# Merged stage: every group's routing stands ahead of the next group's logarithms and mixing

## The reference, cut to what matters

```
no = max(o, u + k);   y = (exp(o-no)*p + exp(u+k-no)*v) / (exp(o-no)*q + exp(u+k-no))
no2 = max(w + o, k);  p, q, o = exp(w+o-no2)*p + exp(k-no2)*v, exp(w+o-no2)*q + exp(k-no2), no2
```

```
probs = softmax(layernorm(x) @ gate.T);  w, idx = top_k(probs, 8);  w = w / sum(w)
out = sum over the chosen e of w_e * (silu(x @ Wgate_e) * (x @ Wup_e)) @ Wdown_e
```

## Time and profile before

| | us |
|---|---|
| median of 3 runs | 2035.82 (2034.09 to 2037.69) |
| the profiled execution | 2036.18 |
| its span, first to last instruction | 2034.5 |
| PE busy | 1671.5 (82%) |
| DVE busy | 1139.8 (56%) |
| POOL busy | 1044.0 (51%) |
| ACT busy | 791.4 (39%) |

### The profile page before, as it was taken

One profiled execution on the slowest core, in us unless ns is written; L12 is line 12 of the kernel. 1 busy time (PEld: TensorE's weight loads), 2 busy tenths in 40 slices (PEclk: granted clock), 3 DMA queues, 4 the chain that ended last, 5 costly groups with the idle time before them and its releaser, 6 DMA issues. The chain is left out here.

```text
span 2034.5 us, 36281 instructions
## 1 busy us (share of the span) xinstructions
PE 1671.5 (82%) x9306; PEld 1233.2 (61%) x9306; DVE 1139.8 (56%) x3459; ACT 791.4 (39%) x2192; POOL 1044.0 (51%) x1023
## 2 busy tenths in 40 slices
PE   7988985888699999999996576564159999999982
PEld 3466663555377777777773233332149988888872
DVE  3122335665544566666665666776425567777774
ACT  3411222222144454554544334333025554445541
POOL 5040006577763333333331267777777666666652
PEclk9999996998899999999997787766579999999996
DMA  8836647993476778778433137334956678888884
GB/s 302 261 95 155 167 126 250 361 333 114 142 286 229 264 278 284 271 274 292 160 131 112 55 112 271 126 125 139 389 164 200 194 245 268 289 269 290 287 266 166
DMA packets 244105, 444.72 MB, mean 219 GB/s; under 512 B 92560, under 2 KB 174608, under 8 KB 241168
## 3 DMA queue, kind: packets, MB, share of 16 engines
q1 hardware_dynamic: 168352, 237.46, 36.4%
q0 software_dynamic: 47856, 147.81, 19.9%
q10 hardware_dynamic: 27712, 57.28, 8.4%
HBM read 281.09 MB, written 237.60 MB: 255 GB/s over the span
## 5 line engine op out<-in xcount | busy, mean ns | idle before, releaser
L1044 PE MATMUL ps<-w_all,h_xT 128*128 x2112 | 551.4, 384 | 0.3 <-ACT h_xT L1328 0.3
L1061 PE MATMUL ps<-w_all,h_hT 89*128 (+1 forms) x1472 | 411.5, 384 | 27.0 <-DVE h_y L1924 24.8
L795 POOL DMA_INDIRECT y_b<-h_y,h_ix x314 | 316.8, 1009 | 164.6 <-issue 112.5
L1044 PEld LDWEIGHTS ps<-w_all,h_xT 128*128 128x128 f32 x2112 | 348.0, 193 | 48.1 <-issue 3.9
L795 POOL DMA_INDIRECT y_a<-h_y,h_ix x208 | 202.2, 972 | 302.0 <-ACT h_y L1361 287.4
L779 POOL DMA_INDIRECT xs_b<-h_x,slot_of x256 | 269.5, 1053 | 160.4 <-DVE slot_of L1755 83.1
L1061 PEld LDWEIGHTS ps<-w_all,h_hT 89*128 89x128 f32 (+1 forms) x1472 | 271.1, 192 | 90.3 <-issue 34.4
L1328 ACT COPY h_xT<-ps 128x256 f32<-128x256 f32 x528 | 194.4, 368 | 196.7 <-PE ps L1037 193.7
L779 POOL DMA_INDIRECT xs_a<-h_x,slot_of x192 | 191.7, 999 | 119.0 <-issue 57.9
L1037 PE MATMUL ps<-ident,h_x 128*128 128x128 f32 x912 | 178.4, 277 | 29.3 <-DMA h_x<-xs_b 29.1
L1037 PEld LDWEIGHTS ps<-ident,h_x 128*128 128x128 f32 x912 | 128.4, 143 | 82.7 <-issue 20.1
(11 more groups left out here) (266 smaller groups left out, 2235.0 us busy)
## 6 DMA issues: line engine op xcount, KB each, us to landing
xs_b<-void_d SPq DMA_DIRECT2D x40, 1128.0 KB
h_x<-xs_b SPq DMA_DIRECT2D x80, 564.0 KB
h_c<-y_a ACTq DMA_DIRECT2D x28, 768.0 KB, 5.3
h_x<-xs_a SPq DMA_DIRECT2D x34, 564.0 KB, 4.2
xs_a<-void_d ACTq DMA_DIRECT2D x16, 1128.0 KB, 13.6
w_all<-in_exp SPq DMA_DIRECT2D x6, 2560.0 KB, 22.2
h_x<-y_b SPq DMA_DIRECT2D x28, 512.0 KB
s_b<-y_b SPq DMA_DIRECT2D x28, 512.0 KB
```

The lines of the kernel that those rows point to most:

```text
L795: pool.indirect_dma_start(y_d[L.name], bass.IndirectOffsetOnAxis(ap=h_ix[:, i % IX:i % IX + 1], axis=0), result_buffer(L, i), None).then_i ...
L1044: m = pe.matmul(ps[:, 2 + s % 2, 0:2 * L.H], h_xT[:, s % 2, c, :], w_all[:, bass.ds(e * L.W + c * 2 * L.H, 2 * L.H)], start=(c == 0), stop ...
L1061: m = pe.matmul(ps[:, 6 + s % 2, 0:D], h_hT[0:w, s % 2, j, :], w_all[0:w, bass.ds(e * L.W + L.up0 + j * D, D)], start=(j == 0), stop=(j == ...
```

## The change

It changes the order of the three lists. In passes 1 to 7 of all engines the routing of group g-1 now stands where group 0's stood: DVE's choice between the two `weight_sums` and its slots ahead of `mixed`; ACT's row steps, turning and exponential around the second `decays`; PE's turning and logits ahead of `past_less_key` and its ranks directly behind. Group 7's routing in pass 8 keeps its order. `last_choices_summed` and `last_choices_added` move from pass 2 to pass 3, and PE's wait in it from `wk_yu` 2 to 3. A wait is added: `states_back(3)` waits for `wk_var` 2. ACT's `key_deviations(2, ...)` stays in pass 3. No instruction of an engine or queue is added or removed by the source except this wait; SP's and POOL's lists are unchanged.

```diff
--- before.py
+++ after.py
@@ -1100,7 +1100,7 @@
 
             def last_choices_summed():
                 pe.wait_ge(k_in, 16)
-                pe.wait_ge(wk_yu, 2)
+                pe.wait_ge(wk_yu, 3)
                 for h in range(2):
                     for k in range(L0.K):
                         m = pe.matmul(ps[:, h, :], ident[:], k_a[:, 2 * h:2 * h + 2, k * D:(k + 1) * D],
@@ -1134,6 +1134,8 @@
                 pe.wait_ge(wk_y, g + 1)
                 if g:
                     pe.wait_ge(wk_yu, g)
+                if g == 3:
+                    pe.wait_ge(wk_var, 2)
                 for j in range(GT):
                     for c in range(KC):
                         m = pe.transpose(ps[:, j // 2, (j % 2) * D + c * P:(j % 2) * D + c * P + P],
@@ -1148,22 +1150,22 @@
                 if g < NG:
                     decays_of(g, 0)
                     decays_of(g, 1)
-                if g == 1:
-                    turned(L1, 0)
-                    logits(L1, 0, e_g1)
+                if 0 < g < NG:
+                    turned(L1, g - 1)
+                    logits(L1, g - 1, e_g1)
                 if g < NG:
                     past_less_key(g, 0)
                     past_less_key(g, 1)
-                if g == 1:
-                    ranks(L1, 0)
-                if g == 2:
+                if 0 < g < NG:
+                    ranks(L1, g - 1)
+                if g == 3:
                     last_choices_summed()
-                if g > 1:
+                if g == NG:
                     turned(L1, g - 1)
                     logits(L1, g - 1, e_g1)
                 if g + 1 < NG:
                     keys_turned(g + 1)
-                if g > 1:
+                if g == NG:
                     ranks(L1, g - 1)
             experts_of_tiles(L1, 2)
             end_stage(pe, "M")
@@ -1456,29 +1458,30 @@
             for g in range(NG + 1):
                 if g < NG:
                     decays(g, 0)
-                if g == 1:
-                    row_logarithms(0)
-                    row_deviations(0)
-                    rows_normalised(0)
-                    results_landed(act, L0)
-                    turned(L1, 0)
+                if 0 < g < NG:
+                    row_logarithms(g - 1)
+                    row_deviations(g - 1)
+                    rows_normalised(g - 1)
+                    if g == 1:
+                        results_landed(act, L0)
+                    turned(L1, g - 1)
                 if g < NG:
                     decays(g, 1)
-                if g == 1:
-                    exponentials_of(L1, 0)
+                if 0 < g < NG:
+                    exponentials_of(L1, g - 1)
                 if g < NG:
                     logarithms(g, 0)
                     logarithms(g, 1)
-                if g > 1:
+                if g == NG:
                     row_logarithms(g - 1)
                     row_deviations(g - 1)
                 if g < NG:
                     shares(g, 0)
-                if g > 1:
+                if g == NG:
                     rows_normalised(g - 1)
                 if g < NG:
                     shares(g, 1)
-                if g > 1:
+                if g == NG:
                     turned(L1, g - 1)
                     exponentials_of(L1, g - 1)
                 if g == 3:
@@ -2126,26 +2129,26 @@
                     residual(g - 1)
                 if g < NG:
                     weight_sums(g, 0)
-                if g == 1:
-                    row_tails(0)
-                    row_scales(0)
-                    less_largest(L1, 0)
-                    chosen_experts(L1, 0)
+                if 0 < g < NG:
+                    row_tails(g - 1)
+                    row_scales(g - 1)
+                    less_largest(L1, g - 1)
+                    chosen_experts(L1, g - 1)
                 if g < NG:
                     weight_sums(g, 1)
-                if g == 1:
-                    slots_of(L1, 0)
-                if g > 1:
+                if 0 < g < NG:
+                    slots_of(L1, g - 1)
+                if g == NG:
                     row_tails(g - 1)
                     row_scales(g - 1)
                 if g < NG:
                     mixed(g, 0)
                     mixed(g, 1)
-                if g == 2:
+                if g == 3:
                     last_choices_added()
                 if g == 4:
                     key_scales(2, slice(NT - GT, NT))
-                if g > 1:
+                if g == NG:
                     less_largest(L1, g - 1)
                     chosen_experts(L1, g - 1)
                     slots_of(L1, g - 1)
```

## The result

| | before | after |
|---|---|---|
| median, us | 2035.55 (2034.09 to 2037.69, 4 runs) | 2057.91 (2054.35 to 2060.95, 4 runs) |
| ratio to before | | 1.0098 (95% interval 1.0074 to 1.0122) |
| profiled execution's span, us | 2034.5 | 2059.2 |
| pass 1 to pass 2, scans of `largest` | 47.60 | 47.60 |
| pass 3 to pass 4 | 43.2 | 56.8 |

The prediction was 2056.5. The profiled execution of after reaches pass 1 3.9 us later than that of before (1120.58 against 1116.67), in stages that the change doesn't touch; its time, 2060.95, is the highest of its four. So times in stage M are compared here from the start of pass 1.

The account below looks back on a forecast made before the run. It saw hand-over idling in the merged stage and POOL's dispatch holding up H1. Passes (285.6) and last choices (10.9) put residual(7) 46.6 us and POOL 22.5 later, H1 20.7 later: 2056.5 us against the median, range 2042 to 2070.

Parts of the forecast that it names:

- Six passes at 47.60: Merged stage: passes 2 to 7 each take pass 1's measured 47.60 us, together 285.6 us.
- The clock case: PE's clock: all at 2.4 GHz, passes of 44.6 us, 2038.5 (chance 0.11); all at 1.2 GHz, 50.9 us, 2076 (0.09).
- The last choices: 3.9 + 6.7 + 0.3: Passes 3 and 4: moved step 3.9 us, exposed key chain 6.7 (at least 5.3), key_scales 0.3; together 10.9 us.
- `residual(7)` 46.6 later: End of pass 7: residual(7) starts at 1462.6 against 1415.97, including 1.8 us waiting for states_back(7).
- POOL 22.5 later: POOL drains each group and idles, only the last two count; first H1 result at 1537.0 against 1514.51.
- The 1.6 us for stores beside the mixing: POOL's group 6: 1.6 us added for four slower issues beside DVE's mixing, at least 0, at most 5.
- The stall at result 14 from 25.2 to 1.1: H1: result 14 wanted at 1546.1, gets its buffer at 1547.2; the 25.2 us stall shrinks to 1.1.
- The sum 20.7 us: Whole kernel: H1's hidden layers end 20.7 us later, the rest moves with them; 2056.5 against the median.
- the 7.90 us per pass: Merged stage: early order costs 7.90 us of idle time per pass, pass 1's 47.60 against pass 7's 39.70.
- the two waits it named: DVE in pass 1: 8.1 us waiting for PE's logits and 4.0 us for the ranks.
- the rival with short passes: Merged stage: POOL's gap is filled and passes take 43 us, giving 2028 us; chance of faster 0.07.

Follow-up runs that it names:

- e1: Changed kernel with ACT's key_deviations(2) moved from pass 3 to pass 4; 2055.53 us, ratio to before 1.0086.
- e3: Changed kernel with three more waited-for stores on SP ahead of the six weight loads, putting off PE's start of H1; 2064.74 us, ratio to before 1.0136.
- e4: Kernel before with three more waited-for stores on SP ahead of the six weight loads, putting off PE's start of H1; 2035.52 us, ratio 1.0001.
- e9: Changed kernel with PE's ranks moved ahead of past_less_key in passes 1 to 7, nothing else; 2030.71 us, ratio to before 0.9967.
- e8: Kernel of e6 with ACT's logarithms also moved ahead of the routing's exponential; 2027.94 us, ratio to before 0.9962.
- e6: Changed kernel with DVE's second weight_sums moved ahead of less_largest and chosen_experts in passes 1 to 7; 2052.22 us, ratio to before 1.0064.

## Why the prediction was right

- *Six passes at 47.60.* Measured 47.6, 47.6, 47.9, 47.3, 47.7 for passes 1, 2, 4, 5 and 6 between scans. The clock case didn't come: the logit matmuls took 3.67 us in pass 7 and the waits stayed 7.8 to 9.0.
- *The last choices: 3.9 + 6.7 + 0.3.* Pass 3 was 9.2 us over 47.6. The exposed wait was 5.37, close to its stated low end of 5.3, since the table load ran ahead of the wait; e1 took it away and gave 5.2 back. With `key_scales` the term was 9.5 us, 1.4 less than the 10.9 of the sum.
- *`residual(7)` 46.6 later.* 45.0; its wait for the transposes was 2.11, taken as 1.8.
- *POOL 22.5 later.* 21.4. That it drains before each group, and that only the last two count, was seen. The 1.6 us for stores beside the mixing measured 2.15 (four stores of 1.30 to 1.88). The count has a small slip: 32 x 1.27 is 40.6, not 40.8.
- *The stall at result 14 from 25.2 to 1.1.* 2.89. Result 14 was wanted 44.6 us later than before, not 46.6, and got its buffer 22.3 later, not 22.5: the difference is the 1.8 us. On POOL's side two errors nearly cancel, which is luck: the first result came 1.1 us earlier than forecast, and the buffer 0.9 us later behind it than in before; why is open. e3 and e4 tested the slack by itself.
- *The sum 20.7 us.* From the start of pass 1 to the end of the span the two profiled executions differ by 20.8 (938.6 against 917.8), so the stages come out as added up. The medians differ by 22.4; the ratio's interval leaves 4.9 us either way, so the 1.7 between them is not clear of noise.

What the prediction did not have was the cause of the 7.90 us per pass in parts, and the 7.90 itself was read from one short pass: old passes 3 to 7 took 43.2, 40.3, 39.8, 41.9 and 39.8 us, 41.0 on the mean, so the early order cost 6.6. The forecast didn't need it, since it counted passes of 47.60. Of the two waits it named, 8.1 and 4.0 us, the second was a matter of order, not of work: PE's order alone (e9) or DVE's and ACT's together (e8, against e6) removes it, and e9's passes average 42.8, 4.8 less than after's 47.6. The first wait was not turned to use in any run: in e8 1.4 us are left of it, but a wait of 5.7 for `w_e` came up, and its passes, 42.7 on the mean, are about as long as e9's. Where the last 1.8 us per pass go, and whether e8 and e9 together would gain more, was not tested. e9 also bears out the price of the rival with short passes: at 43 us a pass it said 2028, and e9 took 2030.71.

## What to carry to other kernels

Work put earlier in the list of an engine that runs in order also goes ahead of everything behind it: for each moved step, list what it waits for and what then waits behind it, on every engine. A consumer with a fixed number of equal jobs (here 256 stores of POOL) loses time mainly by its start and its gaps; find the first point that waits for its last job, and judge the producer's order by that, not by when the producer ends, as long as the other limit keeps its slack (e4 against e3). When a result is made later, look for the wait that had been met a round ago, as `key_deviations` here.

## What the runs showed of the hardware

ACT's table load for a coming function runs before the wait ahead of that function is over: in pass 3 of after the load stands at 1247.51 and the square root at 1267.21, behind a wait of 18.42 us, while in the earlier trace rows the wait had been met and the load of 1.28 us was paid in full. And POOL's stores of the last two groups took a little more than the bare count: from 1453.39 to 1539.84 less 2.57 are 83.9 us for 64, 1.31 each, against 0.97 + 0.30 in the earlier trace rows. Four of them, beside DVE's mixing, took 1.30 to 1.88 us, which is most of the excess.
